# Maxima matmuls of three attention layers issued in twos, one on each half of the array's rows, behind one wait for two free PSUM slots

## What is computed

```python
h = _layernorm(x, ln1_g, ln1_b)
q = (h @ Wq).reshape(Bb, Ss, H, Dh)
k = (h @ Wk).reshape(Bb, Ss, H, Dh)
v = (h @ Wv).reshape(Bb, Ss, H, Dh)
scores = jnp.einsum('bqhd,bkhd->bhqk', q, k) / jnp.sqrt(jnp.float32(Dh))
attn = jax.nn.softmax(scores, axis=-1)
ctx = jnp.einsum('bhqk,bkhd->bqhd', attn, v).reshape(Bb, Ss, Dd)
```

## Time and profile before

| | us |
|---|---|
| median of 3 runs | 2999.33 (2994.53 to 3003.95) |
| the profiled execution | 3007.16 |
| span of its trace, first to last instruction | 3005.1 |
| TensorE busy | 2679.2 (89%) |
| VectorE busy | 1942.2 (65%) |
| ScalarE busy | 1879.1 (63%) |
| GpSimd busy | 399.6 (13%) |

### The profile page before, as it was taken

The page is one execution under the profiler, slowest core; times in us unless marked ns, Lnnn a source line. Parts: engine busy times, 40 slices in busy tenths (PEclk is TensorE's granted clock), DMA queues, the critical chain, the costliest instruction groups (busy, mean ns, idle before and its releaser), DMA issues. The chain is left out here.

```text
span 3005.1 us, 63409 instructions
## 1 busy us (share of the span) xinstructions
PE 2679.2 (89%) x21001; PEld 1136.9 (38%) x21001; DVE 1942.2 (65%) x4035; ACT 1879.1 (63%) x2273; POOL 399.6 (13%) x662
## 2 busy tenths in 40 slices
PE   6788875999999997999599999958999999997998
PEld 2688872222222222444334344422222222223443
DVE  5544447888788884322488778747888888883222
ACT  4222213999889897343256556546999989895432
POOL 1322203111111110000012111101111111110000
PEclk9888866999999999899789999977999999997999
DMA  1000003111111111111111111113111111111211
GB/s 45 1 0 0 0 0 109 36 46 41 35 42 46 43 39 34 64 63 42 67 45 54 48 48 54 45 39 121 34 38 45 46 47 38 36 43 37 71 63 35
DMA packets 93520, 130.71 MB, mean 43 GB/s; under 512 B 17969, under 2 KB 60940, under 8 KB 90828
## 3 DMA queue, kind: packets, MB, share of 16 engines
q1 hardware_dynamic: 85909, 116.73, 12.6%
q10 hardware_dynamic: 7344, 10.32, 1.0%
HBM read 90.28 MB, written 23.89 MB: 38 GB/s over the span
## 5 line engine op out<-in xcount | busy, mean ns | idle before, releaser
L684 ACT ACTIVATE Fprob<-Fs 128x1024 f32<-128x1024 f32 x512 | 507.6, 1032 | 47.5 <-PE Fs L536 35.5
L684 ACT ACTIVATE Hprob<-Hs 128x1024 f32<-128x1024 f32 x512 | 508.1, 1031 | 41.7 <-PE Hs L536 29.2
L761 DVE TENSOR_REDUCE Lmaxes<-Lm 128x1 f32<-128x512 f32 (+3 forms) x640 | 354.5, 604 | 97.2 <-PE Lm L520 62.9
L761 DVE TENSOR_REDUCE Fmaxes<-Fm 128x1 f32<-128x512 f32 x620 | 386.7, 682 | 37.6 <-PE Fm L596 31.7
L761 DVE TENSOR_REDUCE Hmaxes<-Hm 128x1 f32<-128x512 f32 x620 | 387.0, 682 | 31.4 <-PE Hm L596 30.1
L684 ACT ACTIVATE Lprob<-Ls 128x1024 f32<-128x1024 f32 (+7 forms) x384 | 293.7, 778 | 170.9 <-PE Ls L536 105.5
L568 PE MATMUL Fo<-Fprob,Fvh 128*32 128x256 f32 x4096 | 324.9, 395 | 0.3 <-ACT Fprob L684 0.3
L568 PE MATMUL Ho<-Hprob,Hvh 128*32 128x256 f32 x4096 | 323.0, 393 | 0.3 <-ACT Hprob L684 0.3
L536 PE MATMUL Fs<-Fqa,ka 60*128 60x512 bf16 x1024 | 257.0, 388 | 1.6 <-ACT Fprob L684 1.6
L536 PE MATMUL Hs<-Hqa,ka 60*128 60x512 bf16 x1024 | 255.7, 386 | 1.5 <-ACT Hprob L684 1.5
L596 PE MATMUL Lm<-ka,Lqa 60*128 60x512 bf16 (+3 forms) x640 | 190.7, 375 | 31.9 <-issue 10.9
(11 more groups left out here) (445 smaller groups left out, 3937.1 us busy)
## 6 DMA issues: line engine op xcount, KB each, us to landing
FEwb<-FE_weights SPq DMA_DIRECT2D x8, 1024.0 KB, 5.8
HEwb<-HE_weights SPq DMA_DIRECT2D x8, 1024.0 KB
Fvh<-vstack SPq DMA_DIRECT2D x17, 256.0 KB, 2.5
Lvh<-vstack SPq DMA_DIRECT2D x17, 256.0 KB, 2.5
Hvh<-vstack SPq DMA_DIRECT2D x17, 256.0 KB, 2.5
FEw<-in_L_ffn_W SPq DMA_DIRECT2D x16, 256.0 KB, 2.9
HEw<-in_L_ffn_W SPq DMA_DIRECT2D x16, 256.0 KB
Fqa<-F_qparts SPq DMA_DIRECT2D x34, 96.0 KB
```

The source lines that it names most:

```text
L684: nc.scalar.activation(prob[:, :, :].rearrange("p k q -> p (k q)")[:, lo:hi], sps[entry_slot(h, "score", a, n)][:, o:o + hi - lo], ACT.Exp ...
L761: nc.vector.reduce_max(maxes[:, a, t, kb:kb + 1], src[:, 0:n], AX.X).then_inc(max_free, 1)
```

## The change

Items are handed out in twos. An item with an even number `j` in its half is a first, one with an odd number a second; `SECONDS` holds the places of the seconds in `FLAT`. A cut between a first and its second is moved ahead of the first, so both stand ahead of the same entry. The first waits for both slots (`need` is one more than before), the second for nothing; the turn waits for its one slot as before. The row group is now `j % GROUPS`, so a first is on rows 0 to 63 and its second on rows 64 to 127. No instruction is added or taken away but waits.

```diff
+    runs = [BEFORE, len(MAXES[0]) - BEFORE + BEFORE, len(MAXES[1]) - BEFORE]
+    assert all(n % 2 == 0 for n in runs)
+    SECONDS = {sum(runs[:k]) + k + i for k in range(3) for i in range(1, runs[k], 2)}
...
         lead = next(n for n in range(PM + BEFORE + 2)
-                    if all(spent[PLACE[a, "turn"] + 1] - spent[n] + MARGIN <= starts[a] for a in range(2)))
+                    if n % PM not in SECONDS and all(spent[PLACE[a, "turn"] + 1] - spent[n] + MARGIN <= starts[a] for a in range(2)))
...
         upto = [int(np.searchsorted(spent - spent[lead], x)) - lead for x in at[1:]]
+        upto = [n - ((lead + n) % PM in SECONDS) for n in upto]
...
-                    if not (isinstance(c, int) and c <= MSLOTS):
-                        pe.wait_ge(max_free, c - MSLOTS)
+                    first = j == "turn" or j % 2 == 0
+                    need = c - MSLOTS + (1 if first and j != "turn" else 0)
+                    if first and not (isinstance(need, int) and need <= 0):
+                        pe.wait_ge(max_free, need)
...
-                    r = PLACE[a, j] % GROUPS
+                    r = j % GROUPS
```

## The result

The changed kernel takes 3109.83 us (median of 4 runs, 3104.42 to 3112.57), against 3000.36 for the kernel before in the same series (4 runs, 2994.53 to 3003.95). The ratio is 1.0365, with a 95% interval of 1.0343 to 1.0386, so the change costs 109 us. The profiled execution took 3109.72 us, with a span of 3107.7; that is 102.6 us more span than the profiled execution of before, which lay 0.3% over its own median.

What follows compares the result with a forecast made beforehand. It took F and H as bound by TensorE's list. New waits of 5.5 less 3.2 saved gave +2.2 us a head; 70 + 19 (L) - 7 (loop) = +82 on 2999.3 made 3081 us, 8 in 10 within 3015 to 3115.

Steps and rivals of the forecast that it cites:

- The holding time of 1.17: In F and H, from a pair's start to the next pair's earliest start: 0.42 + 0.68 + 0.06 = 1.17 us.
- Fewer slots, -3.2: Per head of F and H, 26 slots for 38 save 2.6 us and three vanished waits 0.7: together -3.2.
- small ones: Pairs in neighbouring entries and scores right behind a difference pair wait slightly longer: +0.6 us a head, between 0 and 1.2.
- Two pairs in one entry, +0.74 four times: At blocks and entries with items on both sides of differences, the second pair waits 0.74 us: +3.0 a head.
- Behind a turn: The pair after a turn comes 1.77 us after the turn's entry starts, for 1.37: 0.39 twice, +0.8 a head.
- behind a paired tile: The next pair may come only after 1.42 us, where it would at 1.11: 0.31 at four places, +1.3 a head.
- The divide: Once a head it keeps VectorE 1.2 us; the second pair behind it waits 1.1 for 0.9: +0.2.
- Overlap, -0.4: Some new waits in a head of F or H fall together, so 0.4 us is taken off their 5.9.
- L, +1.2: Each of L's 16 heads grows by 1.2 us, a middle value between -0.6 and +3.1: +19 in all.
- The loop's turn, -7: Where the loop goes round, a slot is worth double for some 8 us; 13 places give back 0.5 each: -7.
- faster: Rival, chance 0.09: TensorE waits for ScalarE at two-pair places anyway, covering the 1.17 us, so about 2890 to 2950 us.
- Worse by the clock: Rival, chance 0.05: the 0.74 us pauses make TensorE's clock fall, adding a few us a head: about 3130 to 3200.

## Why the prediction was right, and where its sizes were off

The forecast (slower, by the slots' holding time) came about, and 3109.83 lies inside the range, near its upper end. The time is 29 us above the 3081, and the steps show where. The ledger of one head of F, from turn entry to turn entry, in us (sums of the distances of starts, 30 entries in either kernel):

```
entries                      before   after   measured   predicted
2 with a turn                  2.74    3.54     +0.79      +0.8
2 blocks                       4.47    5.45     +0.97      +1.5
6 with differences            10.79   11.66     +0.87      +0.4
20 others                     22.09   21.94     -0.15      -0.15
taken off for overlap                                      -0.4
head                          40.09   42.58     +2.49      +2.2
```

That the head comes within 0.3 of the forecast is in part luck: the blocks grew by 0.5 less than I said and the entries with differences by 0.5 more.

- *The holding time of 1.17* came out as said (its three pieces, as printed, make 1.16): 1.17 from pair to pair, 1.42 behind a paired tile, 1.77 for a turn's entry, 2.28 for the entry with items on both sides (0.89, three slots and 0.74 make 2.27). The run with halved reductions shows it to be the cause in F and H.
- *Fewer slots, -3.2*. The eight entries without items show their 0.89. The saving at entries with differences was too large: I took 0.89 and two slots, 1.32, with 0.1 for the scores. With a pair behind the differences they take 1.51, since ScalarE holds the scores there; with a paired tile ahead of them they take 1.50 (672.20 to 673.70), since the next pair has to wait for VectorE. The earlier trace rows show TensorE's pace in plain entries, and I carried it to entries where another engine sets the length. The "about 0.1" of the small ones is 0.2.
- *Two pairs in one entry, +0.74 four times*. Right around differences. In the block it was put on a wrong base: I said that its 2.24 was "its length without a wait". The rows below show that it had one. In before the block starts at 609.88, a weight load of its third item waits for VectorE, and the second scores come at 610.75, 0.87 after the start. In the kernel with the wait alone, where this wait does not show, the same block has them after 0.62 (617.05, 617.67) and takes 1.99. To 1.98 or 1.99 the 0.74 make 2.73, and 2.71 to 2.73 were measured. The block grew by 0.49.

Timelines of before, PE and its weight loads (PEld):

```profile
610.56 0.09 PEld L596 LDWEIGHTS Fm<-ka,Fqa 60*128 60x128 bf16 x1 [0.51 <-DVE Fmaxes L761]
...
610.75 0.42 PE L536 MATMUL Fs<-Fqa,ka 60*128 60x512 bf16 x2
```

and of the kernel with the wait alone, PE:

```profile
617.05 0.39 PE L598 MATMUL Fm<-ka,Fqa 60*128 60x512 bf16 x1
...
617.67 0.41 PE L536 MATMUL Fs<-Fqa,ka 60*128 60x512 bf16 x2
...
619.04 0.39 PE L591 MATMUL Fm<-pairs,Fqa 60*128 60x512 bf16 x1
```

- *Behind a turn* and *behind a paired tile*: +0.8 came as predicted, and +1.3 as 1.4; the four entries with a paired tile ahead of a plain pair take 1.42 to 1.50 for 1.11.
- *The divide*: +0.2 predicted. Its entry now takes 2.58, with one item less than before, for 2.64; by my sum it was to be 2.42.
- *Overlap, -0.4*: there was none in sum. It was an estimate from walking through the list, with no row of its own.
- *L, +1.2*: measured 1.23. That was a middle value between far bounds; that it met is luck as to its parts, of which the row groups are one that I had not priced.
- *The loop's turn, -7*: nothing came back. I counted some 13 places; the trace has nine, three in each attention. In the three of F the head is longer by 6.4 to 7.2 than its neighbours, for 5.9 to 6.8 before. The timelines of TensorE and VectorE show a wait that I had not thought of:

```profile
788.10 0.39 PE L602 MATMUL Fm<-ka,Fqa 60*128 60x512 bf16 x2 [2.83 <-issue]
...
790.85 2.68 DVE L767 TENSOR_REDUCE Fmaxes<-Fm 128x1 f32<-128x512 f32 x4 [4.69 <-issue]
...
791.60 0.61 PE L602 MATMUL Fm<-ka,Fqa 60*128 60x512 bf16 x2 [1.97 <-DVE Fmaxes L767]
```

and of VectorE before:

```profile
772.90 2.48 DVE L761 TENSOR_REDUCE Fmaxes<-Fm 128x1 f32<-128x512 f32 x4 [4.75 <-issue]
```

VectorE goes round the loop too, 4.69 us without work, and takes up the pair of 788.10 only at 790.85. The next pair waits for it, 1.97 us idle. Before, VectorE stood as long, but a single item came next and found the third slot free (772.46 in the earlier trace rows). I had looked at TensorE's turn of the loop only. That this wait is what took the 7 us is argued and not shown: no run takes it away alone, and at the place shown here the head is longer by 6.65 us than its neighbours, for 6.82 before.

Together: 32 heads at 2.40 in place of 2.2 are 6 us, the loop's turn is about 12 (some 5 lost for 7 gained), L 1. With the 82 that is 101 us, near the 101.7 by which the three attentions grew. Of the other 8 up to 109, 7 are the profiled execution of before, which lay that much over the median.

The rivals: *faster* would need ScalarE to cover the 1.17. It does bound the entries with differences, as that rival said, but this shortened the savings and not the waits. *Worse by the clock* did not come: the clock is 0.99 in the stretch of F, with pauses of 0.57.

The Trainium skill's TensorEngine Tiling (Array Packing), section PSUM Bottleneck, names the emptying of PSUM as what may bound a tiled TensorE. The runs agree that it does here, though by the holding time of three slots and not by VectorE's rate: VectorE is busy 186 of 235 us, and shorter reductions alone took 83 us off.

What stays open: the holding time is shown to be the cause in F and H only. Which places in L carry the 0.51 of the order and the 0.42 of the wait was not taken apart, what the turn of the loop costs was not tested, and a fourth slot was not tried.

## What to carry to other kernels

Before giving work out in larger lots through a ring of few buffers, measure how long a lot holds its buffers from start to release, and compare that with the distance of the next lot in the order of issue. Here three slots and lots of two make that distance 1.17 us, and each nearer neighbour pays the difference. Count a saved instruction as time only in stretches where its engine sets the pace; where another engine does, the work was free and is best left there. A wait and the order that it was written for are one change: tried alone, the wait cost 213 us here and both together 109.

## What the runs showed of the hardware

Three things were new to me. An entry with differences lasts 1.51 us with a pair or with nothing, since its scores wait for ScalarE; that is not to be seen before the items are taken away. VectorE stands 4.69 us idle where the loop goes round, TensorE 2.83; VectorE took up a pair 2.75 us after it started, for 0.42 elsewhere, and TensorE's next pair waited 1.97 for it. And of a slot's 1.17 us less than half follows the columns reduced: 256 columns fewer take off 0.26, so 0.65 would be left with none, an estimate by a straight line through these two points.

TensorE's busy time fell by 95 us while the kernel grew by 109. Its clock did not suffer in mid-head: 0.99 in the stretch of F, with pauses of 0.57.
